# The Hadamard transform of W2 as two TensorE products with a turn by SBUF copies between them

## What is computed

```
x = x + tanh(g_xattn) * wkv(time_decay, time_first, layernorm(x), ctx)
n = layernorm(x)
hidden = silu(n @ W1.T) * (n @ W3.T)        # W1, W3: 2048 x 512
hidden = fwht(hidden) / sqrt(2048)          # along the 2048
x = x + tanh(g_ffn) * (hidden @ W2.T)       # W2: 512 x 2048
```

## Time and profile before

| | |
|---|---|
| median of 3 runs | 1206.31 us |
| the profiled execution | 1207.13 us |
| its span, first to last instruction | 1205.3 us |
| PE, DVE, ACT, POOL busy | 92%, 62%, 19%, 43% |
| granted TensorE clock, mean | 0.967 |
| DMA | 38.8 MB, mean 32 GB/s |

### The profile page before, as it was taken

How to read it: one execution, slowest core, us unless ns; L and a number is a source line. 1 busy time by engine, 2 the same in 40 slices (tenths; PEclk the granted TensorE clock), 3 DMA queues, 4 the chain that set the end, 5 groups by cost and what they waited for, 6 DMA issues and landing times.

```text
span 1205.3 us, 13965 instructions
## 1 busy us (share of the span) xinstructions
PE 1103.6 (92%) x5376; PEld 554.5 (46%) x5376; DVE 748.8 (62%) x811; ACT 226.1 (19%) x296; POOL 514.8 (43%) x401
## 2 busy tenths in 40 slices
PE   6575777787999999999999999999999999999998
PEld 3243666664444444444444444444444444444443
DVE  4977976865596548844793659655884479352112
ACT  4033513211311112012301130111201230110000
POOL 3764732642364335534274337432653437421111
PEclk8796999888999999999999999999999999999999
DMA  6010210010001000010001000100001000000000
GB/s 248 35 70 35 105 71 1 1 70 1 36 1 71 1 35 1 3 68 11 27 1 70 1 35 1 70 2 36 1 20 52 30 6 1 1 1 35 1 1 35
DMA packets 8083, 38.81 MB, mean 32 GB/s; under 512 B 1104, under 2 KB 3280, under 8 KB 3792
## 3 DMA queue, kind: packets, MB, share of 16 engines
q1 hardware_dynamic: 8016, 37.89, 8.2%
HBM read 29.50 MB, written 8.39 MB: 31 GB/s over the span
## 4 chain that ended last, share of the span: by engine, by line
PE 75%; DVE 12%; POOL 5%; issue 5%; ACT 3%; DMA 1%; SPq 0%; DVEq 0%; POOLq 0%; ACTq 0%
PE po L381 8%; PE po L383 8%; PE po L382 8%; PE pg L371 8%; PE pg L373 8%; PE pg L372 8%; PE pl L371 8%; PE pl L372 7%; PE pl L373 7%; DVE v L622 3%; PE pst L347 2%; POOL bv L810 1%; DVE x L635 1%; POOL work L824 1%; PE pst L340 1%
## 5 line engine op out<-in xcount | busy, mean ns | idle before, releaser
L824 POOL TENSOR_TENSOR work<-work 128x512 bf16<-128x512 f32 (+1 forms) x144 | 180.9, 1258 | 453.6 <-DVE work L657 453.6
L649 DVE TENSOR_TENSOR work<-work,pl 128x512 f32<-128x512 f32 (+1 forms) x144 | 89.4, 621 | 357.6 <-PE pl L373 311.4
L381 PE MATMUL po<-work,w2h 128*128 128x512 f16 (+1 forms) x568 | 205.9, 363 | 38.8 <-POOL work L824 24.6
L371 PE MATMUL pg<-xn,w1h 128*128 128x512 f16 (+1 forms) x576 | 208.6, 362 | 35.4 <-ACT work L476 12.8
L476 ACT ACTIVATE work<-pg 128x512 f32<-128x512 f32 (+1 forms) x144 | 79.1, 549 | 728.0 <-PE pg L373 727.1
L372 PE MATMUL pg<-xn,w1h 128*128 128x512 bf16 (+1 forms) x576 | 208.4, 362 | 0.0
L373 PE MATMUL pg<-xn,w1l 128*128 128x512 f16 (+1 forms) x576 | 208.2, 362 | 0.0
L383 PE MATMUL po<-work,w2l 128*128 128x512 f16 (+1 forms) x568 | 206.2, 363 | 0.0
L382 PE MATMUL po<-work,w2h 128*128 128x512 bf16 (+1 forms) x568 | 206.1, 363 | 0.0
L371 PE MATMUL pl<-xn,w3h 128*128 128x512 f16 (+1 forms) x576 | 205.8, 357 | 0.0
L372 PE MATMUL pl<-xn,w3h 128*128 128x512 bf16 (+1 forms) x576 | 205.7, 357 | 0.0
(11 more groups left out here) (83 smaller groups left out, 1184.5 us busy)
## 6 DMA issues: line engine op xcount, KB each, us to landing
xin<-x_t SPq DMA_DIRECT2D x7, 1024.0 KB, 4.9
v<-ctx_t SPq DMA_DIRECT2D x7, 1024.0 KB, 7.0
out_t<-x SPq DMA_DIRECT2D x7, 1024.0 KB, 4.2
x<-w_t SPq DMA_DIRECT2D x5, 1024.0 KB, 4.8
xn<-w_t SPq DMA_DIRECT2D x5, 1024.0 KB, 4.8
work<-w_t SPq DMA_DIRECT2D x2, 1024.0 KB, 8.1
xin<-x_t SPq DMA_DIRECT2D x2, 512.0 KB, 8.8
v<-ctx_t SPq DMA_DIRECT2D x2, 512.0 KB, 12.8
```

The costliest lines, as they stand in the source:

```text
L371: pe.matmul(bank[:, 0:run.n], hi, nh, start=(k == 0), stop=False)
L381: pe.matmul(acc, w2h[:, d, j, :], h, start=first, stop=False, skip_group_check=True)
L649: dve.tensor_tensor(hf[:, j % 2, run.cols], sg[:, j % 2, 0:run.n], pl[:, j % 2, 0:run.n], ALU.mult).then_inc(hidden, 1)
L824: pool.tensor_tensor(hl[:, j % HBUF, run.cols], hf[:, j % 2, run.cols], hh[:, j % HBUF, run.cols], ALU.subtract).then_inc(hid_lo, 1)
```

## The change

W2 comes in by other slices: four groups of 128 partitions (inputs within a block of 128) by four blocks of 512 outputs, `rows`, into the four raw buffers at once. A first product per block j, `mix_rows(j)`, applies the 128 by 128 Hadamard matrix over the partitions (16 products of 512 columns in all), and ACT copies the result to `mixed` (fp32, in the place that w2h and w2l take later). Sixteen DMAs, `turn_rows`, then copy block j, 128 partitions of 2 KB, to the 8 partitions 8j to 8j+7 of `slots` (in the place of the last pieces of w1 and w3), 32 KB in each: a partition then holds 16 of the 128 rows, and the 16 blocks lie over the partitions. A second product, `mix_slots(j)`, with the matrix H16 x I8 / 32 (another 16 of 512 columns) does the transform over the blocks. All of `mix_slots` waits for all 16 copies. ACT rounds its result to f16, DVE clamps it and subtracts it from PSUM for the low part (`slots_hi`, `slots_lo`, 512 columns at a time). The butterflies on DVE and POOL are gone, and so are the W2 splits of 2048 columns. The hidden units come out in another order, which the host's layout of W1 and W3 follows; the factor left, sqrt(1/2), goes into the gate `gt`, by one operation, with a wait on it in `finish`. W1 and W3 share one tensor `w13`, W2 is one tensor with the block outermost.

The list `pieces` has only w1 and w3 (8 pieces); 0 and 1 are split in the prelude, 2 to 7 in slots 1, 2, 3, 5, 6 and 8 of run 0. Loads 0 to 3 wait for `mix_rows`. The orders of SP, TensorE, ACT, DVE and POOL in the prelude are written anew.

```diff
-FLYS = (3, 2, 2, 3)
+PS = 8
+GROUPS = 4
+PER = SLOTS // GROUPS
-SPLIT_SLOT = {1: 6, 2: 7, 3: 8, 5: 9, 6: 10, 8: 11}
-LO_ON_VECTOR = (4, 5, 7, 9, 11)
+SPLIT_SLOT = {1: 2, 2: 3, 3: 4, 5: 5, 6: 6, 8: 7}
+LO_ON_VECTOR = (3, 5, 7)
...
+        rows = [raw[2], raw[3], raw[0], raw[1]]
+        slots = w13[:, WP // 2:, :, :, :].rearrange("p a c k n -> p (a c k n)").bitcast(F32)
...
+            def turn_rows(g):
+                for j in range(PER * g, PER * g + PER):
+                    sp.wait_ge(mixed_out, j + 1)
+                    sp.dma_start(slots[PS * j:PS * j + PS, :], mixed[:, j, :]).then_inc(turned, 16)
...
             load_half(xin, x_in, 0, x_half)
-            load_weights(0)
             sp.dma_start(cc[:, 0:2, :], tdf_in).then_inc(const_loaded, 16)
...
             sp.dma_start(had[:, :, :], had_in).then_inc(had_loaded, 16)
-            load_weights(W2_0)
+            load_rows(0)
+            load_rows(1)
+            load_rows(2)
+            load_half(v, v_in, 0, v_half)
+            load_rows(3)
+            turn_rows(0)
+            load_weights(0)
+            turn_rows(1)
             load_weights(1)
-            load_half(v, v_in, 0, v_half)
-            load_weights(W2_0 + 1)
+            turn_rows(2)
             load_half(xin, x_in, 1, x_half)
             load_half(v, v_in, 1, v_half)
-            for n in range(W2_0 + 2, LATE):
-                load_weights(n)
-            for n in range(LATE, len(pieces)):
+            turn_rows(3)
+            load_weights(2)
+            load_weights(3)
+            for n in range(4, len(pieces)):
                 load_weights(n)
...
+            def mix_rows(j):
+                pe.wait_ge(rows_loaded[j // PER], 16)
+                wait(pe, mixed_out, j - KT + 1)
+                pe.matmul(po[:, j % KT, :], had[:, 0, :], slot_rows(j),
+                          start=True, stop=True).then_inc(had_mm, 1)
+            def mix_slots(j):
+                pe.wait_ge(turned, 16 * SLOTS)
+                wait(pe, w2_lo, j - KT + 1)
+                pe.matmul(po[:, j % KT, :], had[:, 1, :], slot_turned(j),
+                          start=True, stop=True).then_inc(blk_mm, 1)
...
             statistic(Run(0), 0)
+            pe.wait_ge(had_loaded, 16)
+            for j in range(2):
+                mix_rows(j)
             statistic(Run(0), 1)
+            for j in range(2, SLOTS):
+                mix_rows(j)
+            for j in range(4):
+                mix_slots(j)
             statistic(Run(0), 2)
-            hadamard(2, 1)
+            for j in range(4, 8):
+                mix_slots(j)
             statistic(Run(0), 3)
+            for j in range(8, SLOTS):
+                mix_slots(j)
             ffn(Run(0))
...
+            def keep_rows(j):
+                act.wait_ge(had_mm, j + 1)
+                act.copy(mixed[:, j, :], po[:, j % KT, :]).then_inc(mixed_out, 1)
+            def slots_hi(j):
+                act.wait_ge(blk_mm, j + 1)
+                act.copy(w2h[:, j, :], po[:, j % KT, :]).then_inc(w2_hi, 1)
...
             squares(Run(0), 0)
+            for j in range(8):
+                keep_rows(j)
             exps(Run(0), eb, bias_b, exp_b)
             exps(Run(0), ea, bias_a, exp_a)
-            read_hadamard(1)
+            for j in range(8, SLOTS):
+                keep_rows(j)
+            weights_hi(0)
+            weights_hi(1)
+            for j in range(4):
+                slots_hi(j)
             squares(Run(0), 1)
+            for j in range(4, 12):
+                slots_hi(j)
             norm_hi(Run(0))
+            for j in range(12, SLOTS):
+                slots_hi(j)
             ffn(Run(0))
...
+            def slots_lo(j):
+                dve.wait_ge(w2_hi, j + 1)
+                dve.tensor_scalar(w2h[:, j, :], w2h[:, j, :], F16_MAX, -F16_MAX, ALU.min,
+                                  ALU.max).then_inc(w2_clamped, 1)
+                dve.wait_ge(w2_clamped, j + 1)
+                dve.tensor_tensor(w2l[:, j, :], po[:, j % KT, :], w2h[:, j, :],
+                                  ALU.subtract).then_inc(w2_lo, 1)
...
             for k in range(KT):
                 residual(a, k)
-            sums(0, 2)
+            clamp(0)
+            clamp(1)
+            for j in range(4):
+                slots_lo(j)
             centre(a, 1)
-            sums(1, 0)
-            sums(1, 1)
-            clamp(2)
+            for j in range(4, 8):
+                slots_lo(j)
             rsqrt(a, 1, range(NEWTON))
-            clamp(3)
             normalise(a, 1)
+            for j in range(8, 12):
+                slots_lo(j)
             norm_lo(a)
+            for j in range(12, SLOTS):
+                slots_lo(j)
             ffn(a)
...
             for k in range(KT):
                 quotient(a, k)
-            differences(0, 1)
-            differences(0, 2)
+            weights_lo(pool, 0, raw_lo_pool)
+            weights_lo(pool, 1, raw_lo_pool)
             ffn(a)
```

More of the change, by code:

```diff
@@ L137, in flamingo_block @@
         cst_exp, cst_tanh, cst_decay = sem("cst_exp"), sem("cst_tanh"), sem("cst_decay")
-        had_mm = sem("had_mm")
-        had_read = sem("had_read")
-        fly_add, fly_sub = sem("fly_add"), sem("fly_sub")
+        rows_loaded = [sem(f"rows_loaded{g}") for g in range(GROUPS)]
+        mixed_out, turned = sem("mixed_out"), sem("turned")
+        had_mm, blk_mm = sem("had_mm"), sem("blk_mm")
+        w2_hi, w2_clamped, w2_lo = sem("w2_hi"), sem("w2_clamped"), sem("w2_lo")
+        gains = sem("gains")
         raw_hi, raw_clamped = sem("raw_hi"), sem("raw_clamped")
@@ L208, in front_steps @@
                     [(Run(2, 1), step) for step in range(SLOTS) if FRONT2_AT[step] == at])
[L211 to L213 removed]
+        pieces = [(w, p) for p in range(WP) for w in ("w1", "w3")]
         place = [2, 3] + [0, 1] * (len(pieces) // 2 - 1)
         loads = [place[:n + 1].count(place[n]) for n in range(len(pieces))]
[L216 removed]
+        parts = {"w1": (w1h, w1l), "w3": (w3h, w3l)}
         def wait_split(eng, n):
@@ L228, in lo_of, with slot_rows, slot_turned @@
             return parts[pieces[n][0]][1][:, pieces[n][1], :, :].rearrange("p a b -> p (a b)")
-        def split_source(n):
-            q = n - W2_0
-            return fw[q % 2][FLYS[q] % 2] if pieces[n][0] == "w2" else raw[place[n]]
         def weights_lo(eng, n, done):
             eng.wait_ge(raw_clamped, n + 1)
[L237 to L255, removed]
+            eng.tensor_tensor(lo_of(n), raw[place[n]], hi_of(n), ALU.subtract).then_inc(done, 1)
+        def slot_rows(j):
+            return rows[j // PER][:, (j % PER) * D:(j % PER + 1) * D]
+        def slot_turned(j):
+            return slots[:, j * D:(j + 1) * D]
         block = ctx.enter_context(nc.Block())
@@ L478, in weights_hi @@
             def weights_hi(n):
[L479 to L500, removed]
+                act.wait_ge(raw_loaded[place[n]], 16 * loads[n])
+                if pieces[n][1] * 2 >= WP:
+                    act.wait_ge(blk_mm, SLOTS)
+                act.copy(hi_of(n), raw[place[n]]).then_inc(raw_hi, 1)
+            def keep_rows(j):
[4 more added lines that the diff above has]
+                act.copy(w2h[:, j, :], po[:, j % KT, :]).then_inc(w2_hi, 1)
             def front_step(run, step):
@@ L747, in _ @@
             dve.wait_ge(cst_decay, 1)
+            dve.tensor_scalar(gt[:, 3:4], gt[:, 3:4], float(np.sqrt(0.5)), None,
+                              ALU.mult).then_inc(gains, 1)
             a = Run(0)
             centre(a, 0)
-            clamp(0)
             rsqrt(a, 0, range(NEWTON))
             normalise(a, 0)
-            clamp(1)
-            sums(0, 0)
             weigh(a)
@@ L857, in ffn @@
                         last_lo(run, j)
-                        if run.r == 0 and j < 2:
-                            for stage in last_stages[j]:
-                                differences(KT - 1, stage)
                         for ahead, step in front_steps(run, j):
```

97 lines of the change are left out of this document (24 added, 73 removed).

## The result

The changed kernel takes 1225.4 us (median of four executions), the one before 1206.3; the forecast was 1231. One of the four took 2980.2 us for no known reason and is left out of the comparison: the other three lie between 1220.7 and 1227.4, and their ratio to before is 1.0146, 95% interval 1.0109 to 1.0183, which is slower by 1.5%. The profiled execution took 1223.5 us with a span of 1221.7, 16.4 us above the old span.

A forecast was written before the change was run, and what follows sets the result against it. PE bounds the steady part, so only the start counts, where butterflies hold W2 back. Copies end at 18.0 + 7.8 + 16*4.5 + 1.7 = 99.5 us; 48 more put slot 4 24.8 us later: 1231, range 1187 to 1250.

The forecast's parts named there:

- The steady part costs nothing: From slot 4 of the first FFN to the end: unchanged by the diff, zero either way, 1083 us.
- T: Prelude: end of the wait for all 16 turn copies, where `mix_slots` starts; forecast at 99.5 us.
- x1 at 42, 13 us of gain if nothing else is late: Prelude on DVE: without clamps and butterflies ahead, x1 is done at about 42 us, where the old kernel has 55.3.
- 4.5 us a copy, chosen between 0.6 and 10: Each 256 KB turn DMA into 8 partitions: 0.6 us at the wide loads' rate, 10 by partitions written; 4.5 taken.
- The sentence on the Trainium skill's rule: Turn copies: bandwidth follows SBUF ports reached; eight neighbouring partitions reach two, 54 GB/s or 4.8 us a copy, about 1236.
- 7.8 us for 3 MB of loads between the copies: SP's queue: loads of pieces 0 and 1 and second halves of x and v add 7.8 us to T.
- T to slot 4 in 48: From the copies' end through products, second layernorm and splits: slot 0 at T+25.3, slot 4 at T+48, uncertain by 4.
- The sum: Slot 4 at 147.5 us in place of 122.75, 24.8 later: 1207.1 + 24.8 - 0.8 = 1231.
- B: Rival: turn copies as fast as other transfers, 0.6 to 1.3 us each; 1173 to 1180 us; chance 0.13.
- C: Rival: turn copies in between, 1.3 to 2.95 us each; 1180 to 1206 us; chance 0.11.
- D: Rival: turn copies' rate goes with the partitions, 10 us each; 113 us later, 1319 us; chance 0.04.
- E: Rival: copies fast, but the split of the slots bounds, 2 us a slot instead of 0.95; 1196 us; chance 0.04.

The follow-up runs named there:

- both gains together: Changed kernel with copies to 8 partitions at a step of 4 and the second layernorm ahead of the copies' wait: 1182.4 us, ratio to before 0.9798.
- turn_first: Changed kernel with all 16 copies ahead of the loads of pieces 0 and 1 and of the second halves of x and v in SP's list: 1235.6 us.
- wide copies: Changed kernel with each of the 16 copies going to all 128 partitions, 2 KB in each, leaving out the turn: 1175.0 us.

## Why the prediction was right, and where not

- *The steady part costs nothing.* Right. Span less T is 1131.2 us in the changed kernel, 1130.9 with half the bytes, 1130.2 and 1129.6 with the steps of 16 and 4, 1133.2 with 16 neighbours: five values of T from 52 to 91, and the end moves with T to within 4 us. From slot 4 to the end the changed kernel takes 1080.9 us, the old one 1082.6; the forecast said 1083. So a shift at slot 4 is passed on nearly whole, 16.4 of 18.0 us. It is not a law: with both gains together this part took 1085.1, and 4.6 of 5.0 us were lost in it, part of them to a lower granted clock.
- *x1 at 42, 13 us of gain if nothing else is late.* It was 40.7, 14.6 earlier than the 55.3 of the earlier trace rows, and worth nothing, since statistic 2 stood behind the wait for the copies.
- *4.5 us a copy, chosen between 0.6 and 10.* Right in size. At 62 GB/s 256 KB take 4.2 us; in turn_first, from 18.0 to 94.4 less 1.7 of landing, the 16 took 4.7 each. The fast end is real too: the wide copies are it. That the choice met the size is in part luck, since the reason given, a destination a sixteenth as wide, was not the right one: 8 partitions with a step of 4 are as few, and took T to 52.5. What counts is which partitions they are. The sentence on the Trainium skill's rule had it, with 4.8 us.
- *7.8 us for 3 MB of loads between the copies.* The size was about right where it could be measured, the way to it was not. It took the queues for one resource that copies and loads share. Copies to 8 partitions hold half of them, and the loads run on the rest at the same time (share 0.54, then 1.06), but slow the copies there from 62 to some 49 GB/s, 7 us in turn_first. Moving the loads out from between the copies took 9.8 us off T with the step of 16 and 8.2 with 16 neighbours. For the changed kernel itself the term stays open: with it T was forecast at 99.5, without it it would be 91.7, and 90.5 and 103.2 were measured.
- *T to slot 4 in 48.* Measured 50.2 (slot 0 at T+27.2 for 25.3, then 23.0 for 22.7). The unit prices held: 0.29+0.69 us a slot, 0.9 a product. What was missed is mostly how late PE gets to its last four products: it waits 5.2 us for the first `slots_lo` after the normalise, and runs them at the lower clock at first (5.62 us for four where 3.6 is usual; granted clock 0.50 from 112.0 to 114.5).
- *The sum.* 24.8 us for slot 4, measured 18.0: T came 9.0 earlier than forecast, and the way from T to slot 4 took 2.2 more. The two misses cancel in part. The 1231 lies between the two medians measured, 1225 and 1235.
- *The rivals.* B, copies as fast as others, is what the wide copy does (1175, forecast 1173 to 1180), and fell for the real one. C, 1.3 to 2.95 us a copy, is where the step of 4 lies (1.6 by its T, 1185). D, the price in proportion to the partitions, fell with the step of 4. E, the split as the new bound, fell as priced: the slots go at 0.93 us each on DVE.

## What to carry to other kernels

A DMA's price hangs on which SBUF partitions it writes: with the same bytes and the same number of partitions, a step of 4 in place of neighbours took this kernel from 1.5% above the old one to 1.7% below the old one measured beside it. Before a reordering through SBUF copies is costed, look which partitions one copy reaches, and whether the layout leaves a free choice of them, as the Hadamard factor does here. And what stands in an engine's list behind a wait that it does not need is late with it: the front moved ahead of the copies' wait took 10 us off the way from T to the end by order alone. Where the wait had become short, with the step of 4, the same move is not shown to gain anything.

## What was not expected of the hardware

- Copies with 8 destination partitions keep the DMA share at 0.53 to 0.54, with 16 at 1.08: half of the queues do such a copy. With 8 neighbours the other half takes loads at the same time, and the copies fall from 62 GB/s to some 49 meanwhile; with the step of 16 the copies' own packets fall from 101 to 106 GB/s to 69 to 75.
- The same program has its copies done at 90.5 us in one profile and at 103.2 in another, with medians of 1225.4 and 1234.9 us, while the kernel before, without such copies, differs by 1 us between them (1206.3 and 1207.2). Ten runs of the kernel with the front first, on one chip, lie between 1207.7 and 1227.8 us. The cause was not found.
- 16 neighbours and 8 partitions with a step of 16 have the same reach and run at 122 and 104 GB/s. Why the step of 16 stays lower is open.
